# A transformer layer on one core: the order of weight loads and layer norms in the first V projection is changed

## The reference, cut to what matters

```python
x = x + attention(layernorm(x))      # x: (B=2, S=1024, H=1024)
x = x + ffn(layernorm(x))

# attention
qkv = x @ attn_qkvw + attn_qkvb      # (H, 3H)
probs = softmax(q @ k.T * hd ** -0.5)
out = (probs @ v) @ attn_ow + attn_ob

# ffn
y = (silu(x @ W_gate.T) * (x @ W_up.T)) @ W_down.T

# layernorm: (x - mean) / sqrt(var + 1e-5), no scale, no shift
```

## Time and profile before

| | us |
|---|---|
| median of 3 runs | 3305.98 |
| lowest and highest of them | 3303.16, 3307.39 |
| the profiled execution | 3301.68 |
| its span, first to last instruction | 3300.1 |

### The profile page before, as it was taken

The page is one execution under the profiler, slowest core; times in us unless marked ns, Lnnn a source line. Parts: engine busy times, 40 slices in busy tenths (PEclk is TensorE's granted clock), DMA queues, the critical chain, the costliest instruction groups (busy, mean ns, idle before and its releaser), DMA issues.

```text
span 3300.1 us, 38853 instructions
## 1 busy us (share of the span) xinstructions
PE 3178.2 (96%) x14464; PEld 2484.8 (75%) x14464; DVE 2017.3 (61%) x3098; ACT 1452.6 (44%) x2679; POOL 802.8 (24%) x599
## 2 busy tenths in 40 slices
PE   6999999988999999999899999999999999999999
PEld 5767777766777676776667888888888788888887
DVE  5788888988898888989884332332333423233324
ACT  1477777777777777777571111111111211111111
POOL 1224333333343343334332111010101010101010
PEclk8999999999999999999999999999999999999999
DMA  2434343442433423335447611111121411111111
GB/s 99 129 104 135 91 122 87 130 145 78 124 99 97 136 80 109 113 98 159 137 123 229 202 58 58 58 39 39 60 68 45 174 56 51 39 55 47 52 51 51
DMA packets 146028, 315.90 MB, mean 96 GB/s; under 512 B 24944, under 2 KB 58864, under 8 KB 142256
## 3 DMA queue, kind: packets, MB, share of 16 engines
q1 hardware_dynamic: 145840, 313.42, 30.6%
HBM read 228.41 MB, written 84.41 MB: 95 GB/s over the span
## 4 chain that ended last, share of the span: by engine, by line
PE 83%; DVE 13%; ACT 1%; DMA 1%; issue 1%; SPq 1%; POOL 0%; DVEq 0%; ACTq 0%
PE ps L650 15%; PE ps L651 15%; PE ps L652 15%; PE ps L716 6%; PE ps L735 5%; PE ps L747 5%; PE ps L752 5%; PE ps L805 5%; PE ps L806 5%; PE ps L807 5%; DVE pl L1059 4%; DVE mx L1037 4%; DVE wl L1009 2%; PE ps L677 1%; SPq L1183 1%
## 5 line engine op out<-in xcount | busy, mean ns | idle before, releaser
L874 ACT ACTIVATE pu<-ps 128x512 f32<-128x512 f32 x1024 | 616.1, 602 | 385.2 <-PE ps L735 382.1
L1037 DVE TENSOR_REDUCE mx<-ps 128x1 f32<-128x512 f32 x1024 | 697.6, 685 | 129.7 <-PE ps L716 119.0
L1137 POOL TENSOR_TENSOR pl<-pu,ph 128x512 fp32r<-128x512 f32 x315 | 425.4, 1350 | 980.8 <-ACT ph L875 979.6
L875 ACT ACTIVATE ph<-ps 128x512 fp32r<-128x512 f32 x1024 | 614.5, 600 | 0.0
L1059 DVE TENSOR_TENSOR pl<-pu,ph 128x512 fp32r<-128x512 f32 x709 | 564.2, 796 | 61.9 <-ACT ph L875 58.3
L650 PE MATMUL ps<-x2h,gh 128*128 128x512 f32 x1376 | 535.4, 389 | 0.8 <-DVE x2l L1003 0.8
L652 PE MATMUL ps<-x2l,gh 128*128 128x512 f32 x1376 | 535.3, 389 | 0.0
L651 PE MATMUL ps<-x2h,gl 128*128 128x512 f32 x1376 | 535.3, 389 | 0.0
L1099 DVE TENSOR_TENSOR hf<-ps,sg 128x512 f32<-128x512 f32 (+1 forms) x88 | 60.9, 692 | 694.5 <-PE ps L652 685.9
L716 PE MATMUL ps<-kst,qst 96*128 96x512 f32 x1024 | 419.4, 410 | 38.8 <-DVE mx L1037 37.4
L735 PE MATMUL ps<-qst,kst 98*128 98x512 f32 x1024 | 411.2, 402 | 4.2 <-ACT ph L875 3.9
(11 more groups left out here) (91 smaller groups left out, 4600.2 us busy)
## 6 DMA issues: line engine op xcount, KB each, us to landing
wraw<-in_wqkv SPq DMA_DIRECT2D x24, 1024.0 KB, 5.2
qst<-q_d SPq DMA_DIRECT2D x192, 128.0 KB, 3.0
kst<-k_d SPq DMA_DIRECT2D x192, 128.0 KB, 3.1
graw<-in_wg SPq DMA_DIRECT2D x44, 512.0 KB, 4.6
graw<-in_wu SPq DMA_DIRECT2D x42, 512.0 KB, 3.5
draw<-in_wd SPq DMA_DIRECT2D x42, 512.0 KB, 3.9
q_d<-stg SPq DMA_DIRECT2D x64, 256.0 KB, 2.4
k_d<-stg SPq DMA_DIRECT2D x64, 256.0 KB, 2.3
```

The source lines that it names most:

```text
L874: e.activation(pu[sl][:, :], bk[:, :], ACT.Exp, scale=SCALE).then_inc(s["a_p"], 1)
L875: e.activation(ph[sl][:, :], bk[:, :], ACT.Exp, scale=SCALE).then_inc(s["a_ph"], 1)
L1037: e.reduce_max(mx[:, j % 2, t, half:half + 1], ps[2 + bank_of["a", j, t, half]][:, :], AX.X).then_inc(s["v_mx"], 1)
```

## The change

The steps are the same, but for one more layer norm step. What changes is their order in the list, and how tiles are grouped for the layer norm: `FIRST` gives the groups, and tiles 0 and 1 are now groups of their own. The load of V's weights is issued behind x's tile 0, ahead of tiles 1 to 3. The transposes of tile 0, with their splits, come ahead of V's weight splits, and those of tile 1 behind them. Q's weights are loaded (`loaded(1)`) ahead of the norm of tiles 2 and 3, and that norm comes behind the splits of tile 1. In the loop V(t) comes ahead of the transposes of tile t+2.

```diff
+FIRST = [(0,), (1,), (2, 3), (4, 5), (6, 7)]
...
-    def pair(t0):
-        step("norm", t0)
-        for t in (t0, t0 + 1):
+    def norm(i):
+        step("norm", i)
+        for t in FIRST[i]:
             if t + 4 < TT:
                 step("xload", t + 4)
...
-    for t in range(4):
+    step("xload", 0)
+    loaded(0)
+    for t in range(1, 4):
         step("xload", t)
-    pair(0)
-    pair(2)
-    loaded(0)
+    norm(0)
+    norm(1)
+    transposed(0, 0)
     while later:
         due()
+    transposed(0, 1)
+    loaded(1)
+    norm(2)
     first_v = v_group(0)
     for t in range(TT):
-        if t % 2 == 0 and 2 <= t < TT - 2:
-            pair(t + 2)
-        transposed(0, t)
-        for _ in range(KT if t else 0):
+        for _ in range(KT):
             while next(first_v, 0) is None:
                 due()
             due()
+        if t in (1, 3):
+            norm(3 + t // 2)
+        if t + 2 < TT:
+            transposed(0, t + 2)
     run(first_v)
```

More of the change, by code:

```diff
@@ L489, in of_norm, with of_rstd @@
     return n * TT + t + 1
-def of_rstd(n, t0=0):
-    return t0 // 2 + 1 if n == 0 else TT // 2 + n
+def of_rstd(n, i=0):
+    return i + 1 if n == 0 else len(FIRST) + n
 def of_o(n, half):
@@ L813, in act_program @@
                 if what == "norm":
-                    t0, = at_
-                    act.wait_ge("v_var", of_rstd(0, t0))
-                    e.activation(rs[:, 1, t0:t0 + 2], rs[:, 0, t0:t0 + 2], ACT.Sqrt).then_inc(s["a_sd"], 1)
+                    i, = at_
+                    z = slice(FIRST[i][0], FIRST[i][-1] + 1)
+                    act.wait_ge("v_var", of_rstd(0, i))
+                    e.activation(rs[:, 1, z], rs[:, 0, z], ACT.Sqrt).then_inc(s["a_sd"], 1)
                 elif what == "rstd":
@@ L926, in dve_program, with reciprocal_root @@
             stat = 0
-            def reciprocal_root(n, z):
+            def reciprocal_root(n, z, i=0):
                 nonlocal stat
@@ L932, in reciprocal_root @@
                 e.tensor_scalar(v, mv[:, n, z, 1], EPS, None, ALU.add).then_inc(s["v_var"], 1)
-                dve.wait_ge("a_sd", of_rstd(n, z.start))
+                dve.wait_ge("a_sd", of_rstd(n, i))
                 e.reciprocal(r, sd).then_inc(s["v_st"], 1)
@@ L946, in dve_program @@
                 if what == "norm":
-                    t0, = at_
-                    tiles = (t0, t0 + 1)
+                    i, = at_
+                    tiles = FIRST[i]
                     for t in tiles:
@@ L958, in dve_program @@
                     dve.wait_ge("v_st", stat)
-                    reciprocal_root(0, slice(t0, t0 + 2))
-                    dve.wait_ge("v_rq", of_rstd(0, t0))
+                    reciprocal_root(0, slice(tiles[0], tiles[-1] + 1), i)
+                    dve.wait_ge("v_rq", of_rstd(0, i))
                     for t in tiles:
```

## The result

The changed kernel took 3292.76 us in the median of 6 runs (3290.94 to 3293.76), the kernel before 3306.68 in 6 runs beside it (3301.29 to 3308.39): a ratio of 0.9962, 95% interval 0.9949 to 0.9974. That is 13.9 us won, and 3292.8 had been forecast. The profiled execution of the changed kernel took 3291.49, its span was 3289.8, 10.3 shorter than that of before (3300.1).

What follows compares the result with a forecast made beforehand. DVE's early work and late weight loads were taken to hold up TensorE ahead of the Q projection; 15.7 - 0.8 - 1.3 - 0.4 = 13.2 us won, so the median goes from 3305.98 to 3292.8, range 3288.5 to 3299.

Steps and rivals of the forecast that it cites:

- The 15.7: Most that could be won, in us: the Q projection starts at 53.0 against 68.70, before any deductions.
- the rivals with late transfers: Before V(0): x's tile 1 2 us late, 3294.4 (chance 0.07); or V's weights late, V(0) at 22, 3298 (0.03).
- those with the low clock throughout: TensorE slow through the V stretch, no gain, 3306.6 (chance 0.05); or slow into Q's products too, 3317.6 (0.02).
- the clock's 0.8: Deduction at V(3): TensorE may run it at the low clock, 0 to 1.8 us net, taken as 0.8.
- the transfers' 0.4: Deduction before V(0): early transfers may share bandwidth and bring x's tile 1 late, costing up to 2 us; taken 0.4.
- POOL's 1.3: Deduction for DVE instructions lengthened by POOL's weight pieces beside the first norms: between 0 and 3.3 us, taken as 1.3.
- Q's first two low parts: Step on DVE behind the norm of tiles 2 and 3: two pieces of Q's weights, priced at 1.20 us.
- the rival "ports": Short DVE instructions at tiles 1 to 3 also queue behind POOL's pieces: 3.3 us instead of 1.3, 3294.8; chance 0.13.
- V(3) at its worst and the loop 2 worse: Rival: V(3) at low clock and the attention loop up to 2 us worse, put at 3296.6; chance 0.06.
- The remainder: Length from the Q projection to the end, claimed to stay as before, 3231.4 us within 3.
- The low stretch at 120 to 140: Low clock around 130 us in the attention loop; the shift may remove it or bring it back, up to 2 us.

Runs made afterwards that it cites:

- experiment 1: The kernel before with only the load of V's weights moved ahead of x's tiles 1 to 3; median 3296.28 us, ratio 0.9978.
- experiment 4: The changed kernel with ACT instead of POOL making the high parts of the first two weight groups; median 3291.96 us, ratio 0.9962.
- experiment 3: The changed kernel with the load of Q's weights issued behind the norm of tiles 2 and 3; median 3299.28 us, ratio 0.9987.

## Why the prediction was right, point by point

**The road and its end.** Right: the change acts ahead of Q only, and DVE is the pacer without a hole. It stands still for no more than 0.27 at a time (the square root on ACT) from 5.49 to 46.90. The 15.7 that this way could give at most, less 2.2, are the 13.5 won at Q; 2.5 had been taken off. The medians moved by 13.9, 14.4 and 13.0 in three comparisons, so what is won at Q arrives at the end. V(0) at 17.11 rules out the rivals with late transfers (tile 1 late by 2 us, or V(0) at 22), and V(3) at 36.69 those with the low clock throughout.

**The size.** That 13.2 came so near to 13.5 is in part luck, since errors of opposite sign met. Of the 2.5 taken off, the clock's 0.8 and the transfers' 0.4 were not needed in the first profile; POOL's 1.3 were 2.1, x's tile 0 came 0.2 late and TensorE took 0.3 more from V(5) to Q, while DVE's norms were 0.3 cheaper than priced. The median, 3292.76 for 3292.8, hit closer than the method can: three comparisons give 13.0 to 14.4.

**V(0).** 17.11 for 16.7: x's tile 0 came 0.2 later (5.49), and tile 0's norm took 4.29 for the 3.87 put down. Of it, `rq` (0.41 for 0.16) and the normalization (1.09 for 0.81) were 0.5 longer beside POOL, and the rest was 0.1 cheaper. Tile 1's norm took 3.67 for 3.85.

**Transfers.** Taken 0.4, measured 0, apart from tile 0's 0.2. V's weights let POOL begin at 8.03. Tile 1's statistics followed tile 0's normalization at once, at 9.78. Its data arrive at 9.02 in experiment 1, and the group of one hides that. Q's weights, issued at 17.08, let POOL begin at 22.46, 5.4 later, where 4.8 had been put; DVE asked for the first high part only at 24.65, so nothing waited for them.

**DVE beside POOL.** The right mechanism with the wrong size: taken 1.3, measured 2.1 by the lengths of the instructions and 1.9 by experiment 4's V(3). The two normalizations of tiles 2 and 3 cost 0.7. The term that was too small is the price of Q's first two low parts: they were put at 1.2, as if POOL were through, and took 2.02, since POOL had begun late and was itself drawn out. The trace of the kernel before had that price, in a line that the forecast didn't use:

```profile
34.36 2.10 DVE L1009 TENSOR_TENSOR wl<-wraw,wh 128x512 fp32r<-128x512 f32 x2 [3.11 <-POOL wh L1129]
```

POOL's four pieces of Q's weights took 3.67, where they took 2.37 in experiment 1 with DVE idle or at statistics:

```profile
7.80 2.37 POOL L1130 TENSOR_SCALAR wh<-wraw 128x512 fp32r<-128x512 f32 x4 [7.36 <-DMA wraw<-in_wqkv]
```

The measured price lies between the forecast's and that of the rival "ports" (1.3 and 3.3), nearer to the forecast's. In this profile only one short instruction was longer, tile 0's `rq` (0.41). But what the rival describes does happen: in the changed kernel's second profile POOL began at 21.73, beside the chain of tiles 2 and 3, and two short instructions took 0.54 and 0.53, while the low parts took only 1.27. The sum is nearly the same there (31.04 from tile 0's arrival to V(3), for 31.20): what POOL costs shifts with the moment at which the weights are in.

The Trainium skill, in "SBUF — State Buffer", section "Who interferes with whom", has VectorE and GpSimd as the only two that share ports, and ScalarE as one that never waits. Experiment 4 agrees: the same pieces on ACT took 2.19 for four, and no DVE instruction beside them was longer than its like.

**The clock.** Taken 0.8 for V(3), within 0 to 1.8. In the first profile it cost nothing: V(3) ran fast. In the next it did what had been described. V(3) was slow until 39, reached the next transposes at 40.61 instead of 39.27, and the wait before V(5), 0.98 in the first profile and gone in this one, took up all but 0.1 of it. Its windows:

```profile
35.00:37.50 2.50, 1.34 (x7) 1.22 (x6) 2.50 (x6) 1.09 (x3) 0.00 (x0) 0.69 0.00 0
37.50:40.00 2.50, 2.50 (x16) 2.50 (x15) 2.50 (x5) 0.00 (x0) 0.00 (x0) 0.63 0.00 0
```

In experiment 4 it cost 2.3, of which 1.1 showed at Q, and that is where its gain went. In the changed kernel's three profiles V(0) was slow for most of its length, and V(1) in part in two of them, at no cost, as foretold: DVE was later. One price among the rivals was added up wrongly: with V(3) at its worst and the loop 2 worse it is 3292.8 + 2 + (1.8 - 0.8) = 3295.8, not 3296.6, for 0.8 had been taken already.

**The remainder.** Foretold as 3231.4 within 3, on the ground that the list of steps is one. It was 3234.6, 3.2 more and so just outside, and the ground had a gap: this length is not a constant of the program. It varies by 6.4 for one kernel. The low stretch at 120 to 140 that the prediction named did go (0.83 in the earlier trace rows, 1.00 now), but others came, at 700 for one:

```profile
120.00:140.00 20.00, 19.37 (x113) 15.50 (x113) 18.61 (x36) 14.55 (x29) 5.46 (x4) 1.00 0.33 89
...
700.00:720.00 20.00, 17.15 (x81) 12.56 (x79) 16.87 (x25) 13.87 (x26) 8.88 (x8) 0.83 0.63 188
```

That the forecast of the median held owes something to the fact that it was made as a difference from the median of before, whose runs average over this.

## What to carry to other kernels

When a start-up stage waits for a load, ask for each load what the queue holds in front of it, and then what the engine behind it does in the meantime: here the load alone was worth 7.2 us, all the rest of the change on top of it 6.3, and one line of that rest 6.9 if put wrong. These numbers don't add up, for each is measured against another kernel. A step that is to run beside another on DVE and POOL is priced with both drawn out, and moving it to an idle ACT removes that price. A single profile is no measure of a gain of a few microseconds behind the stage that was changed; read the gain at the point where both programs become the same, and take the rest from medians.

## What the runs showed of the hardware

- The column of the granted clock is no proof of full speed at the start. The first eight transposes, at 9.92, take 1.94 us while the column says 1.00 from 10 to 12; at 39.67 eight of them take 1.03. The Trainium skill, in "TensorE: Matmul & The Clock Gate", section "What's actually happening", has 1.2 GHz as the level of an idle engine, which agrees.
- Which product falls to half speed differs between executions of one kernel: V(3) was fast in two profiles of the changed kernel and slow in one, and had waited 1.16 us in all three.
- POOL's four weight pieces took 2.37 us with DVE idle or at statistics (experiment 1), and beside other work of DVE 2.80 (V's in the changed kernel), 3.23 (Q's in experiment 3) and 3.67 (Q's in the changed kernel): POOL is drawn out as DVE is.
- ACT copies four weight pieces of 128x512 in 2.19 us (experiment 4), no slower than POOL with DVE idle.
